# Second attention of a two-layer block rescheduled between batches: centred value weights, decays issued by themselves, scans ahead of the denominators

## What is computed

```
f_log = log_sigmoid(f_t); m_new = max(f_log + m, i_t)
C = exp(f_log + m - m_new) * C + exp(i_t - m_new) * k_t v_t^T      # n the same with k_t alone
h = (qs @ C) / (max(|qs @ n|, exp(-m_new)) + EPS)
h_norm = (h - mean(h)) * rsqrt(var(h) + EPS) * gamma               # over the 32 values of the head
y = (sigmoid(x @ Wog.T) * h_norm) @ Wout.T
```

## Time and profile before

| | |
|---|---|
| timed runs, median (lowest to highest) | 1043.09 us (1038.96 to 1043.93) |
| profiled execution, span | 1000.6 us (the page gives no end-to-end time for it) |
| busy share PE, DVE, ACT, POOL | 84%, 74%, 39%, 44% |
| mean granted PE clock | 0.899 |
| second attention, from first transposes to the first matmul of the feed-forward | 571.4 to 821.4 us |

### The profile page before, as it was taken

How to read it: one execution, slowest core, us unless ns; L and a number is a source line. 1 busy time by engine, 2 the same in 40 slices (tenths; PEclk the granted TensorE clock), 3 DMA queues, 4 the chain that set the end, 5 groups by cost and what they waited for, 6 DMA issues and landing times. The chain is left out here.

```text
span 1000.6 us, 18851 instructions
## 1 busy us (share of the span) xinstructions
PE 841.5 (84%) x6846; PEld 710.9 (71%) x6846; DVE 741.7 (74%) x1561; ACT 393.7 (39%) x760; POOL 441.3 (44%) x582
## 2 busy tenths in 40 slices
PE   5789898898668968878889599999999989899963
PEld 4677777775557757667777478788887878788763
DVE  5678887876648635996565578888778677999894
ACT  2333433342343353334333264554345553333320
POOL 3123333322342347777774835665643313333332
PEclk9999999997869979999999877987679879999986
DMA  7000000000000158899986523111110000000001
GB/s 252 2 2 12 12 12 2 12 12 12 12 11 2 44 159 263 267 292 311 307 258 198 172 61 101 49 47 52 48 31 0 0 1 1 1 1 22 22 1 42
DMA packets 58315, 77.69 MB, mean 78 GB/s; under 512 B 9698, under 2 KB 50925, under 8 KB 58232
## 3 DMA queue, kind: packets, MB, share of 16 engines
q1 hardware_dynamic: 30968, 40.92, 13.0%
q0 software_dynamic: 9856, 18.92, 6.6%
q10 hardware_dynamic: 17408, 16.78, 4.9%
HBM read 61.88 MB, written 23.07 MB: 85 GB/s over the span
## 5 line engine op out<-in xcount | busy, mean ns | idle before, releaser
L520 POOL DMA_INDIRECT work<-xnd,rows_at x128 | 133.3, 1041 | 49.6 <-issue 32.6
L940 PE MATMUL ZO<-parts 128*128 128x256 f32 x288 | 88.6, 308 | 25.4 <-DVE parts L1531 7.5
L446 POOL TENSOR_SCALAR_AFFINE_SELECT work<-work 128x256 f32<-128x256 f32 x128 | 52.9, 438 | 121.4 <-ACT work L653 121.4
L437 POOL TENSOR_SCALAR veps<-mv 128x2 f32<-128x2 f32 x64 | 18.7, 293 | 189.6 <-DVE mv L1492 189.3
L1907 DVE TENSOR_TENSOR work<-work,S 64x256 f32<-64x256 f32 x128 | 54.2, 424 | 59.9 <-ACT work L779 55.2
L653 ACT ACTIVATE work<-S 128x768 f32<-128x768 f32 x64 | 51.6, 811 | 95.7 <-PE S L1014 95.7
L941 PE MATMUL ZO<-parts 128*128 128x256 f32 x288 | 82.9, 288 | 0.0
L942 PE MATMUL ZO<-parts 128*128 128x256 f32 x288 | 82.8, 288 | 0.0
L940 PEld LDWEIGHTS ZO<-parts 128*128 128x128 f32 x288 | 56.1, 195 | 33.9 <-issue 13.3
L940 PE MATMUL S<-xr,parts 128*128 128x512 f32 x192 | 79.1, 412 | 0.8 <-issue 0.8
L619 POOL TENSOR_TENSOR parts<-work,parts 128x512 fp32r<-128x512 f32 x32 | 44.1, 1378 | 80.3 <-ACT parts L896 80.3
(11 more groups left out here) (316 smaller groups left out, 2468.9 us busy)
## 6 DMA issues: line engine op xcount, KB each, us to landing
yd<-work ACTq DMA_DIRECT2D x64, 256.0 KB
raw<-in_experts SPq DMA_DIRECT2D x74, 192.0 KB, 3.5
work<-in_experts SPq DMA_DIRECT2D x36, 192.0 KB
lg_all<-in_experts SPq DMA_DIRECT2D x18, 192.0 KB
raw<-in_ffn SPq DMA_DIRECT2D x2, 1536.0 KB, 7.2
xnd<-attn_w SPq DMA_DIRECT2D x8, 256.0 KB, 2.1
shd<-work SPq DMA_DIRECT2D x8, 256.0 KB, 2.3
work<-xnd,rows_at POOLq DMA_INDIRECT x128
```

What stands on the lines that cost most here:

```text
L446: last = pool.affine_select(out=diagonal, in_=diagonal, compare_op=ALU.is_ge, fill=0.0, base=0, pattern=[[0, 2], [1, P]], channel_multipli ...
L520: pool.indirect_dma_start(xg[:, i % RING, b, :], None, xnd[:], bass.IndirectOffsetOnAxis(ap=rows_at[:, 2 * i + b:2 * i + b + 1], axis=0), ...
L940: pe.matmul(dst, a(0), b(0), start=start, stop=False, skip_group_check=True)
```

## The change

Seven things are done.

- The value weights `wv1` are centred per head once (`second_constants`), so that the values, and with them each head's output, have mean zero without a subtraction; the mean, the subtraction and its chain leave DVE. The square goes to ACT (`squares`), and the product with the output gate reads PSUM.
- These constants, the norm weights in `wo1`, the selector `sel1` and the rest of `gA` are made in steps 24 to 27 of the expert loop, where they were made ahead of the attention.
- PE's decays become a function of their own (`decays`) that waits for the exponentials of the pair before, not for its weights; the decays of the first pair of the next batch are issued between the two groups of queries and keys. `dec` gets a third buffer.
- Queries and keys of the second group go to bank `T1`, the gate columns to `S[1]`; the second group is copied inside the batch, after the first pair.
- On DVE the scans and gate rows of the next batch go ahead of the denominators; signs are turned so that one scaling of the scans goes.
- The product with the head factor goes ahead of the first weights, its transposes on PE ahead of the first values, and the low half of the final input to the end of the batch.
- ACT loads its tables by explicit instructions, one after the input copy, one after the tanh.

```diff
+        QK = (S[0], T1)
@@ ACT, gate_functions
                 act.activation(gf, T1[32:32 + H1, 0:T], ACT.Tanh, bias=bfg15, scale=1.0 / CAP).then_inc(s["c_tanh"], 1)
+                act.preload_act_table_set("natural_log_exp_and_others")
                 act.wait_ge(s["c_tanh"], b + 1)
@@ ACT
+            def squares(b):
+                act.wait_ge(s["c_pv"], b + 1)
+                act.activation(sq.rearrange("p t (h e) -> p t h e", e=DV1), both_rows[:, :, :, 0:DV1], ACT.Square
+                               ).then_inc(s["c_sq"], 1)
...
-                    if h >= 2:
-                        act.wait_ge(s["c_w"], b * H1 + h - 1)
-                    act.activation(dec[h % 2][:, 0:256], S[2 + h % 2][:, 0:256], ACT.Exp, bias=gcol[:, 0, h:h + 1])
+                    if h >= 3:
+                        act.wait_ge(s["c_w"], b * H1 + h - 2)
+                    act.activation(dec[h % 3][:, 0:256], S[2 + h % 2][:, 0:256], ACT.Exp, bias=gcol[:, 0, h:h + 1])
...
-                    if h == 3 and not first:
-                        head_rows_copy(b)
+                    if h == 1:
+                        query_copies1(b, 1)
+                        if not first:
+                            head_rows_copy(b)
                     if h == (7 if first else 5) and not last:
                         input_copy1(b + 1)
+                        act.preload_act_table_set("exp_and_others")
                 if not last:
                     gate_functions(b + 1)
+                squares(b)
                 output_sigmoid(b)
@@ PE, projections
-                for g in range(2):
-                    for w, o in ((wq1, 0), (wk1, T)):
...
+                queries_keys(b, 0)
+                gate_columns(b)
+                decays(b, 0)
+                queries_keys(b, 1)
@@ PE
+            def decays(b, pair):
                 if pair:
-                    pe.wait_ge(s["c_w"], b * H1 + 2 * pair)
-                for h in heads:
+                    pe.wait_ge(s["c_dec"], b * H1 + 2 * pair)
+                else:
+                    pe.wait_ge(s["c_v"], b + 1)
+                    pe.wait_ge(s["c_oe"], b + 1)
+                for h in (2 * pair, 2 * pair + 1):
...
+            def scores1(b, pair):
+                heads = (2 * pair, 2 * pair + 1)
+                if pair:
+                    pe.wait_ge(s["c_w"], b * H1 + 2 * pair)
+                else:
+                    pe.wait_ge(s["c_em"], b + 1)
+                if pair % 2 == 0:
+                    pe.wait_ge(s["c_k"], b * 2 + pair // 2 + 1)
@@ PE, mlstm
                     if p < H1 // 2:
+                        if p:
+                            decays(b, p)
                         scores1(b, p)
-                    if p == 1 and not first:
+                    if p == 0 and not first:
                         head_rows(b)
+                    if p == 3 and not (first or last):
+                        gates(b + 1)
                     if p:
                         values1(b, 2 * p - 2)
@@ DVE, expert loop
+                if 24 <= i < 28:
+                    second_constants(i - 24)
@@ DVE
+            def second_constants(n):
+                values = wv1.rearrange("p c (h e) -> p (c h) e", e=DV1)
+                if n == 0:
+                    dve.wait_ge(s["w_c"], 144)
+                    chr_(dve.tensor_reduce(vmean, values, AXX, ALU.add))
+                    chr_(dve.tensor_scalar(vmean, vmean, 1.0 / DV1, None, ALU.mult))
+                if n == 1:
+                    dve.tensor_tensor(values, values, bc(vmean.unsqueeze(2), [P, KC * H1, DV1]), ALU.subtract)
+                if n == 2:
+                    for c in range(KC):
+                        dve.tensor_scalar(wo1[:, c, :], wo1[:, c, :], gam[:, c:c + 1], None, ALU.mult)
...
+                if n == 3:
+                    dve.tensor_copy(sel1, bc(eye1[:].unsqueeze(2), [P, H1, P]))
+                    dve.tensor_copy(gA, bc(ident[:, 127:128], [P, T])).then_inc(s["c_const"], 1)
@@ DVE, scans
-                dve.tensor_scalar(gi, gi, CAP, None, ALU.mult)
-                ch(dve.tensor_scalar(gls, gls, -1.0, None, ALU.mult))
-                dve.tensor_tensor_scan(gF, ones1, gls, 0.0, ALU.mult, ALU.add)
-                ch(dve.tensor_tensor_scan(gm, gls, gi, 0.0, ALU.add, ALU.max))
+                ch(dve.tensor_scalar(gi, gi, -CAP, None, ALU.mult))
+                dve.tensor_tensor_scan(gF, ones1, gls, 0.0, ALU.mult, ALU.subtract)
+                ch(dve.tensor_tensor_scan(gm, gls, gi, 0.0, ALU.add, ALU.min))
@@ DVE, mlstm
+                if not first:
+                    head_product(b - 1)
                 pair(0)
+                key_value_copies(b, 1)
...
-                dve.wait_ge(s["c_pv"], b + 1)
+                if not last:
+                    scans(b + 1, ch)
+                    gate_rows(b + 1, ch)
+                dve.wait_ge(s["c_sq"], b + 1)
...
                 dve.tensor_tensor(den, den, em, ALU.max).then_inc(s["c_den"], 1)
-                means = mu.rearrange("p (t h) -> p t h", t=2)
-                ch(dve.tensor_reduce(means, both[:, :, :, 0:DV1], AXX, ALU.add))
-                ch(dve.tensor_scalar(mu, mu, 1.0 / DV1, None, ALU.mult))
                 sqf = sq.rearrange("p t (h e) -> p (t h) e", e=DV1)
-                ch(dve.tensor_tensor(hc.rearrange("p t (h e) -> p t h e", e=DV1), both[:, :, :, 0:DV1],
-                                     bc(means.unsqueeze(3), [P, 2, H1, DV1]), ALU.subtract))
-                ch(dve.tensor_tensor(sq, hc, hc, ALU.mult))
                 dve.tensor_reduce(hv, sqf, AXX, ALU.add).then_inc(s["c_hv"], 1)
+                dve.wait_ge(s["c_eo"], b + 1)
+                dve.tensor_tensor(hc.rearrange("p t (h e) -> p t h e", e=DV1), both[:, :, :, 0:DV1],
+                                  eo.rearrange("p t (h e) -> p t h e", e=DV1), ALU.mult).then_inc(s["c_hc"], 1)
                 if not last:
-                    scans(b + 1, ch)
-                    gate_rows(b + 1, ch)
+                    gate_columns(b + 1)
                     key_value_copies(b + 1, 0)
-                    gate_columns(b + 1)
-                    key_value_copies(b + 1, 1)
-                dve.wait_ge(s["c_eo"], b + 1)
-                ch(dve.tensor_tensor(hc, hc, eo, ALU.mult))
...
+                if not first:
+                    final_input_low(b - 1)
```

More of the change, by code:

```diff
@@ L270, in build @@
         em = view([P, 2, H1])
-        dec = [view([P, 384]) for _ in range(2)]
+        dec = [view([P, 384]) for _ in range(2)] + [dec2]
         wt = [view([P, 384]) for _ in range(4)]
@@ L1352, in gate_columns @@
                         o = (2 * i + t) * H1
[L1353 removed]
+                        last = pe.transpose(S[1][:, o:o + H1], src[:, t * P:(t + 1) * P], ident[0:H1, 0:H1])
                 last.then_inc(s["c_gT"], 1)
[L1356 to L1357 removed]
+            def decays(b, pair):
                 if pair:
[L1359 to L1360 removed]
+                    pe.wait_ge(s["c_dec"], b * H1 + 2 * pair)
[3 more added lines that the diff above has]
+                for h in (2 * pair, 2 * pair + 1):
                     dc = S[2 + h % 2]
@@ L1414, in mlstm @@
                     if p == (3 if first else 2) and not last:
-                        pe.wait_ge(s["c_em"], b + 1)
                         input_transposes1(b + 1)
-                    if p == (4 if first else 3) and not last:
+                    if p == 4 and first:
                         gates(b + 1)
@@ L2034, in mlstm @@
                 pair(3)
-                if not first and b + 2 < NB:
-                    moe_sum(b + 2, ch, range(3, TOPK))
                 if not first:
+                    if b + 2 < NB:
+                        moe_sum(b + 2, ch, range(3, TOPK))
                     final_input_norm(b - 1)
@@ L2076, in _ @@
             gate_columns(0)
-            for g in range(2):
-                key_value_copies(0, g)
+            key_value_copies(0, 0)
             for b in range(NB):
```

76 lines of the change are left out of this document (34 added, 42 removed).

## The result

The changed kernel takes 1037.6 us (median of 20 runs, 1030.23 to 1044.01), the kernel before 1043.68 (20 runs beside them): ratio 0.994, 95% interval 0.9921 to 0.9959, that is 4 to 8 us less, about 6. Forecast was 1034, between 1019 and 1050.

A forecast was written before the change was run, and what follows sets the result against it. VectorE was taken as each batch's floor, with TensorE's clock setting the excess. Middle batches -9.4, batch 6 -2, last batch -2.5, batch 0 +4.5, last stage 0: -9.4 against the median 1043.09, 1034 us; range 1019 to 1050.

The forecast's parts named there:

- batch 0, to batch 1's boundary: Scans first make batch 0's sum of squares 5.2 us later, passed on through GpSimd's gathers; +4.5 taken.
- four middle batches: Batches 2 to 5: 28.6 us each, 114.4 against 123.82 before, -9.4.
- batch 6: VectorE has less work there, but scans come to wait about 2.5 us for the log; -2 us.
- From D to the head factor: From D (VectorE starts denominators; scans after the change): sum of squares out at D+4.30, GpSimd's factor 4.7 us later.
- The head product waiting for GpSimd one to two us at every boundary: Sign of being right: VectorE's product with the head factor waits one to two us for GpSimd at each batch boundary.
- first weights to the next D: Rest of a batch on VectorE: 17.2 us at TensorE's full clock, the waits for output rows gone.
- The clock: TensorE's clock falls after its wait for first weights, slowing output rows by 1.7 us; over 0.85 in most batches if right.
- One sign of being wrong: Listed signs: middle-batch scans waiting for the log, batch 0's sum of squares at 610 or earlier, batches over 30 us.
- the clock falls as before: Rival, chance 0.25: TensorE still waits about 1 us for the head product at the same place; +1.8, 1045 us.
- VectorE as the bound: VectorE gives each batch's floor, 26.9 us after the change; what lies over it comes with TensorE's clock.
- Table loads: ScalarE's gate functions: a load costs 1.29 us by the trace; the log is done about 2 us before VectorE asks.
- Constants: About 4 us of VectorE work moved into four expert steps costs nothing; without that cover, 4.

The follow-up runs named there:

- second profile of the kernel before: The kernel before, unchanged, profiled again beside the follow-up runs: 1040.6 us, span 1038.9.
- all orders mended and the waits filled: Changed kernel; batch 0: sums before scans, second keys before gate columns; projections before final input's transposes; useless matmuls ahead of last scores and values: 1021.2 us, 0.9772.
- kernel before with a filled wait: Kernel before with 17 useless small matmuls ahead of TensorE's wait for the first weights in batches 1 to 7: 1031.32 us, 0.989.
- sums-first run: Changed kernel with batch 0's square, denominators and sum of squares issued ahead of batch 1's gate functions and scans: 1029.36 us, 0.9851.

## Why the prediction was right, and where it was not

The time was right; half of the reason was not. That it came out 3.6 us from the forecast is in part luck: the largest term was 6.3 us off, as much as the whole change, and the batch after gave 1.8 of it back. Term by term, against the second profile of the kernel before:

| term | forecast | measured |
|---|---|---|
| batch 0, to batch 1's boundary | +4.5 | +4.4 |
| four middle batches | -9.4 (28.6 each) | -3.1 (28.31 each) |
| batch 6 | -2 | -3.8 |
| last batch, to the last stage | -2.5 | -2.1 |
| last stage | 0 | +1.35 |
| sum | -9.4 | -3.3 in this pair of profiles; about -6 by the timed runs |

*The middle batches* are the mis-sized term. Their new length was forecast well, their old one was not: 123.82 us for four, with one of 34.95, was taken as the base; here they take 116.39, and no batch is over 29.9. I had named the 34.95 as the work of the clock and yet counted it as typical. That makes 7.4 us too much; the new length being 0.3 a batch less than forecast gives 1.2 back.

*From D to the head factor* was right: the sum of squares ends at D+4.28 (778.68 to 782.96), forecast 4.30, and the factor is done 4.07 later (4.7 taken, bounds 3.6 to 5.1). The lower bound took VectorE for quiet in batch 0; it was so only until 611.51, a small part of GpSimd's steps. The square takes 0.60 on ScalarE, the gate on the value product 0.68 from PSUM (0.69 taken).

*The head product waiting for GpSimd one to two us at every boundary* was wrong. It starts at D+8.67 without waiting, since VectorE had been held for the gate columns. I had TensorE at the scores near D+9; with the clock down over the projections it delivers them for first weights at D+10.25 (9.7 forecast). The other part, first weights to the next D, is 16.98 (17.2). GpSimd was done at 787.03, 0.3 us before the product, so its wait lay right behind: with all orders mended and the waits filled it comes back (0.28 to 2.10 us at five of six boundaries).

*The clock.* That waiting precedes the fall in the middle batches, and that the fall sets what lies over the floor, was right and is now shown by runs: filling the wait gave 0.989 in the old order, 0.986 in the new. Not every fall has such a wait: in batch 0 of the changed kernel the clock, back at 1.00 since 638 us, fell again near 641 with no wait over 0.30 us. What I missed is that the reschedule doesn't end the fall but moves it, from behind the first weights to behind the last scores, where TensorE waits 0.95 to 0.99 us in each of batches 2 to 5; the clock is over 0.85 in four of the last six batches. One sign of being wrong did show: batch 2 took 30.31 us, at a clock of 0.78, after VectorE had waited 4.84 us for the gate columns at the end of batch 1. The wait for the output rows did go in batches 2 to 5 (3.25 us are left in the last batch), as forecast; the two waits at the boundary took its place. This is the rival called "the clock falls as before", in another place. The Trainium skill, TensorE: Matmul & The Clock Gate, section HAM oscillation — how this bites in real kernels, advises arranging a loop so that TensorE doesn't stop between its matmuls, there for transfers, so that it stays warm. The trace agrees where the wait is for VectorE: filling it took 11 us off the stage of the kernel before.

*VectorE as the bound* was wrong for the old order at the clock that it ran at: there 0.9 us less work gave nothing. At a clock of 1.00 it was right: batches 3 and 5 of the kernel before with a filled wait take 26.74 to 26.87 us with all of the old work, and VectorE is busy 25.2 to 25.3 of them and waits no longer than 0.28 at a time. That is the floor of 26.9 that I forecast for the new order; what less work for VectorE would give there, no run shows. In the new order the work before the sum of squares costs 2.0 us a batch when it is put back, but part of that came by TensorE's clock, so that the path through VectorE is argued there and not shown.

*Batch 0* was right in size and place: the sum of squares starts 35.5 us after the first scans, 30.3 before, +5.2, with the log at 31.9 in both. That most of it passes on through GpSimd's gathers is shown by the sums-first run. The wait for the log is 4.33. The new wait of TensorE for the gate rows (3.02 us of idle time), which the bounds had, came too, and the clock fell behind it; without it the log came 1.6 us earlier and VectorE's wait for it stayed at 4.34.

*Table loads* take 1.28 us (774.21 to the exponential at 775.50; the instruction before ends 0.02 ahead of the load) and the middle batches don't wait for the log: so the sum was right to go by the earlier trace rows. The 2.66 us of the Trainium skill, ScalarE: Activation LUTs, section What ACT_TABLE_LOAD costs, is not what this case shows. *Constants* in the expert stage cost nothing that can be seen: the first scans start at 620.9 to 629.0 us in the runs with them, at 623.8 and 628.1 in the two later profiles without them.

What stays open: why the last stage took 1.35 more; how much of the difference between -3.3 in the profiles and -6 in the timed runs is the expert stage, whose end varies by 8 us over the later profiles (the two executions compared took 1040.6 and 1040.8 us, so nearly the same time); and what decides in which batch the clock falls.

## What to carry to other kernels

Before work is taken off the busiest engine, take a little of it away, or fill the other engine's wait, and look which of the two moves the time: here VectorE was busy 25 of 28 us and yet not the bound, until TensorE's wait was filled. Two edits that gain nothing alone can gain together, so try them both ways before one is dropped. When an order is changed, do the first pass of a loop by itself, since what is early in the steady state can be late there (9 us of the stage).

## What was not expected of the hardware

With seventeen matmuls of 128x128 bf16 (1.12 us in all) ahead of a wait of 1.21 us, the granted clock of batches 3 and 5 read 1.00, where it had been 0.88. And a TensorE that is busy can stay at the half level for long: in batch 0 of the changed kernel it had no wait over 0.3 us from 643 to 655 us, in matmuls of 33 to 256 columns, and the clock read 0.50 all the while; it rose during the sixteen matmuls of 256 columns that followed.
